# Graph attention on one core: a padded K/V table, and three transfers issued after the table's stores

## The reference

```python
q, k, v = x @ Wq + bq, x @ Wk + bk, x @ Wv + bv          # each as (6250, 8, 16)
scores = sum(q[dst] * k[src], -1) * 16 ** -0.5 + (edge_attr @ We + be)
e = exp(scores - segment_max(scores, dst)[dst])
probs = e / (segment_sum(e, dst) + 1e-10)[dst]
agg = segment_sum(probs[:, :, None] * v[src], dst)
out = layernorm(x + agg @ Wo + bo)
```

## Time and profile before

| what | value |
|---|---|
| time, median of 3 runs | 2090.21 us (2089.79 to 2093.34) |
| time of the profiled execution | 2089.85 us |
| its span | 2088.0 us |
| granted TensorE clock over the span | 0.597 |
| busy: PE, DVE, ACT, POOL | 1462.7, 1441.3, 869.7, 1532.9 us |
| gathers (L481) | 1564, mean 968 ns busy |

### The profile page before, as it was taken

How to read it: one execution, slowest core, us unless ns; L and a number is a source line. 1 busy time by engine, 2 the same in 40 slices (tenths; PEclk the granted TensorE clock), 3 DMA queues, 4 the chain that set the end, 5 groups by cost and what they waited for, 6 DMA issues and landing times.

```text
span 2088.0 us, 31893 instructions
## 1 busy us (share of the span) xinstructions
PE 1462.7 (70%) x8917; PEld 921.8 (44%) x8917; DVE 1441.3 (69%) x3420; ACT 869.7 (42%) x3368; POOL 1532.9 (73%) x1578
## 2 busy tenths in 40 slices
PE   5567767667676777767667787776667776768766
PEld 4344544444443544444435454444444443545443
DVE  5466777766766676767667676766676776767766
ACT  0143435444443444344434444443444343434444
POOL 4777777777777777777777777777777777777770
PEclk8555556665656565566555555656565566655555
DMA  7544444444444444444444444444444444444430
GB/s 292 194 126 127 128 152 126 150 127 147 131 133 142 130 150 127 151 129 151 128 150 129 149 128 148 131 132 143 129 151 128 151 127 151 127 152 126 138 116 9
DMA packets 115285, 290.07 MB, mean 139 GB/s; under 512 B 45719, under 2 KB 53644, under 8 KB 108068
## 3 DMA queue, kind: packets, MB, share of 16 engines
q0 software_dynamic: 75072, 205.10, 32.9%
q1 hardware_dynamic: 37324, 76.25, 10.6%
q10 hardware_dynamic: 2712, 6.67, 0.9%
HBM read 276.38 MB, written 11.51 MB: 138 GB/s over the span
## 4 chain that ended last, share of the span: by engine, by line
POOL 71%; issue 23%; PE 2%; DVE 2%; DMA 1%; ACT 0%; ACTq 0%; POOLq 0%; DVEq 0%
POOL kv_buf L481 71%; PE q_banks L1079 1%; DMA kv_table<-kv_buf 1%; DMA kv_buf<-kv_table,src_i 0%; PE ps_t L1079 0%; PE ps_w L1079 0%; DVE wv L779 0%; PE ps_a L1152 0%; DMA bias_row<-in_L_gnn_bv 0%; ACT distance L546 0%; DVE prod L758 0%; DVE seq_f L854 0%; DVE seq_b L859 0%; PE ps_a L1204 0%; PE ps_a L1205 0%
## 5 line engine op out<-in xcount | busy, mean ns | idle before, releaser
L481 POOL DMA_INDIRECT kv_buf<-kv_table,src_i x1564 | 1514.0, 968 | 495.8 <-issue 473.7
L1116 PE MATMUL q_banks<-q_blk,onehot_t 64*128 64x128 f32 x3128 | 433.3, 418 | 525.6 <-DVE prod L758 520.9
L758 DVE TENSOR_TENSOR prod<-q_banks,kv_buf 128x512 f32<-128x512 f32 (+1 forms) x392 | 269.3, 687 | 564.7 <-issue 467.2
L1116 PEld LDWEIGHTS q_banks<-q_blk,onehot_t 64*128 64x128 f32 x3128 | 335.3, 288 | 639.4 <-issue 636.1
L537 ACT ACTIVATE onehot_t<-ps_t 128x256 f32<-128x256 f32 (+1 forms) x392 | 149.2, 380 | 990.4 <-PE ps_t L1102 978.9
L1152 PE MATMUL ps_a<-wv,onehot 128*64 128x136 f32 x3128 | 418.2, 414 | 60.6 <-ACT onehot L552 58.1
L546 ACT ACTIVATE distance<-iota_n,neg_rel 128x64 f32<-128x64 f32 x1564 | 416.2, 341 | 0.0
L1152 PEld LDWEIGHTS ps_a<-wv,onehot 128*64 128x64 f32 x3128 | 267.3, 202 | 154.1 <-ACT onehot L552 87.6
L779 DVE TENSOR_TENSOR wv<-kv_buf,ps_w 128x512 f32<-128x512 f32 (+1 forms) x392 | 264.4, 675 | 6.0 <-PE ps_a L1152 3.8
L769 DVE TENSOR_REDUCE score<-prod 128x32 f32<-128x512 f32 (+1 forms) x392 | 264.9, 676 | 4.0
L552 ACT ACTIVATE onehot<-distance 128x256 f32<-128x256 f32 (+1 forms) x392 | 163.0, 416 | 12.4
(11 more groups left out here) (144 smaller groups left out, 1417.6 us busy)
## 6 DMA issues: line engine op xcount, KB each, us to landing
edge_f<-in_edge_blk SPq DMA_DIRECT2D x55, 1024.0 KB, 6.2
kv_buf<-kv_table,src_i POOLq DMA_INDIRECT x1564, 3.7
kv_table<-kv_buf ACTq DMA_DIRECT2D x12, 512.0 KB, 5.0
xt_blk<-in_x_t SPq DMA_DIRECT2D x114, 32.0 KB, 4.3
out<-y_out SPq DMA_DIRECT2D x114, 32.0 KB
kv_buf<-in_x_perm SPq DMA_DIRECT2D x5, 512.0 KB, 8.8
codes<-code_table SPq DMA_DIRECT2D x108, 10.5 KB
code_table<-kv_buf SPq DMA_DIRECT2D x1, 1344.0 KB, 6.0
```

Of the source, the lines that this page charges most:

```text
L481: pool.indirect_dma_start(kv_buf[:, b % NBUF, t, :], None, kv_table, bass.IndirectOffsetOnAxis(ap=src_i[:, column:column + 1], axis=0)).th ...
L758: dve.tensor_tensor(prod[:, q % 2, 0:n * D].rearrange("p (k j d) -> p j k d", j=2, d=D), q_banks[:, :, 0:n // 2 * D].rearrange("p j (k d) ...
L1116: one = pe.matmul(ps_q[j][:, k * D:(k + 1) * D], onehot_t[own, q % 2, k * P:(k + 1) * P], q_blk[own, b % QBUF, :], start=True, stop=True)
```

## The change

The last group gets 128 nodes in place of 106, so the table has `NR` = 6272 rows; the 22 extra rows hold what zero features give and no edge points at them. The last chunk of x is loaded 640 columns wide in place of 618. On SP the loads and the store behind `src` now wait for all table stores, and stand in another order: order check, code table, distances. POOL no longer waits for the code table before its first gather, but for the codes to be computed; the wait for the code table's store now stands before those steps of block 0 whose tiles lie in the codes' place.

```diff
-    GROUPS += [(n, 1, min(P, N - n), False) for n in range(N // (QUAD * P) * QUAD * P, N, P)]
+    GROUPS += [(n, 1, P, False) for n in range(N // (QUAD * P) * QUAD * P, N, P)]
+    NR = GROUPS[-1][0] + GROUPS[-1][1] * P
...
-    XCHUNKS = [(0, min(N, QUAD * P))] + [(lo, min(N, lo + XCHUNK)) for lo in range(QUAD * P, N, XCHUNK)]
+    XCHUNKS = [(0, min(NR, QUAD * P))] + [(lo, min(NR, lo + XCHUNK)) for lo in range(QUAD * P, NR, XCHUNK)]
...
-        kv_table = nc.dram_tensor("kv_table", [N, KV], F32).ap()
+        kv_table = nc.dram_tensor("kv_table", [NR, KV], F32).ap()
...
-        xt = in_kv(P, 1, 0, N)
+        xt = in_kv(P, 1, 0, NR)
...
-        row_code = kv_buf[0:ROWS, 0, 16:28, :].rearrange(...)
+        CODE_HOME = (16, 28)
+        row_code = kv_buf[0:ROWS, 0, CODE_HOME[0]:CODE_HOME[1], :].rearrange(...)
...
             sync.dma_start(src_i[:, :], src_blk).then_inc(s_src, 16)
+
+            for i in range(STAGES):
+                sync.wait_ge(s_table[i], TABLE_DONE[i])
+            sync.dma_start(chk_i, dst_chk).then_inc(s_chk, 16)
             sync.wait_ge(s_rowcode, ROWCODE["rest"])
             sync.dma_start(code_table.rearrange("k (r e) -> r k e", e=ROW), row_code).then_inc(s_codetable, 16)
-            sync.wait_ge(s_staged, len(HALVES))
-            sync.dma_start(chk_i, dst_chk).then_inc(s_chk, 16)
             sync.dma_start(dst_i[:, :], dst_blk).then_inc(s_dst, 16)
             sync.wait_ge(s_setup, SETUP["codes"])
             sync.wait_ge(s_codetable, 16)
...
             def gather(b):
                 for g, (t0, t1) in enumerate(STEP[b]):
+                    if b == 0 and t0 < CODE_HOME[1] and t1 > CODE_HOME[0]:
+                        pool.wait_ge(s_codetable, 16)
...
             for i in range(STAGES):
                 pool.wait_ge(s_table[i], TABLE_DONE[i])
-            pool.wait_ge(s_codetable, 16)
+            pool.wait_ge(s_rowcode, ROWCODE["rest"])
             gather(0)
...
-         x_t[:, quads:N]], axis=1)
+         x_t[:, quads:N + -N % P]], axis=1)
```

More of the change, by code:

```diff
@@ L165, in graph_attention @@
         found = sb("found", [1, 4])
-        assert T * KV >= N and T >= max(STAGES * QUAD, 16) and 2 * (NT + 1) <= 2 * EPAIRS * P
+        assert T * KV >= NR and T >= max(STAGES * QUAD, 16) and 2 * (NT + 1) <= 2 * EPAIRS * P
         assert ROW + 1 <= 8 * KV and KNOWN * ROW <= 12 * 2 * KV
@@ L173, in in_kv @@
             return kv_buf[0:parts, half, slot:slot + -(-(n + at) // KV), :].rearrange("p a b -> p (a b)")[:, at:at + n]
-        xt = in_kv(P, 1, 0, N)
+        xt = in_kv(P, 1, 0, NR)
         row_i = in_kv(ROWS, 0, 0, ROW + 1).bitcast(I32)
         row_sq = in_kv(ROWS, 0, 8, ROW)
-        row_code = kv_buf[0:ROWS, 0, 16:28, :].rearrange("p a b -> p (a b)").bitcast(BF16)[:, 0:KNOWN * ROW].rearrange(
+        CODE_HOME = (16, 28)
+        row_code = kv_buf[0:ROWS, 0, CODE_HOME[0]:CODE_HOME[1], :].rearrange("p a b -> p (a b)").bitcast(BF16)[:, 0:KNOWN * ROW].rearrange(
             "p (k e) -> p k e", k=KNOWN)
```

## The result

| | before | after |
|---|---|---|
| time, median of 20 runs each | 2090.31 us (2087.79 to 2094.34) | 2082.78 us (2080.29 to 2090.67) |
| ratio | | 0.9966, 95% interval 0.9959 to 0.9973 |
| profiled execution, its span | 2089.85, 2088.0 us | 2082.24, 2080.4 us |
| mean of a gather | 968 ns | 968 ns |
| granted TensorE clock | 0.597 | 0.603 |

A forecast was written before the change was run, and what follows sets the result against it. POOL issuing 1564 gathers in a row was taken as the bound, so the first gather's start counts. Terms -8.2 (start), -0.8 (first gather) and +1.5 (stretch) sum to -7.5 us on 2089.85: 2082.4 us, range 2079.5 to 2088.5.

The forecast's parts named there:

- What bounds the kernel: POOL issuing 1564 gathers one behind another, 1987.7 of 2088.0 us; the change touches the first gather's start.
- Last store and what stands in front: Padded store with transfers behind it lands in 3.3 us, not 11.49; gathers start at 36.5, not 44.66: -8.2 us.
- at worst as the twelfth now: Bound on the last table store: it takes 6.9 us and lands at 38.9, so gathers start only 4.9 us earlier.
- First gather, -0.8: POOL's first gather takes 0.95 us in place of 1.72, as VectorE is then idle and not in L733.
- What runs beside gathers, +1.5: VectorE's L727, L733 and L740, 4.6 us in all, now fall among gathers and stretch them; bounds 0 and 4.6.
- Waits moved on POOL: Code table lands at 43.5 us, gather 17 needs it at 56: 13 us of cover, so no cost.
- Moved on SP: Later check, code table and distances put the flag at 48.4 to 50.6 us, first multiply about 62; no cost.
- The room of 30 us: Slack before POOL waits for a used slot: 40.8 us now, 30 left with earlier gathers and later consumers.
- Late landing: Rival: backlog isn't the code table's alone, table done at 38.9 us; -4.2 us, 2085.7 us; chance 0.12.
- no effect: Rival: the gain at the start is lost before the end, for instance by POOL stalling; 2089 us; chance 0.08.
- full blocking at 4.6 us: Rival: POOL is held for all of L727, L733 and L740; -4.4 us, 2085.4 us; chance 0.12.
- The slower case: Rival: gathers meet VectorE's SBUF instructions in another phase, stretch grows by half, 14 us; 2096.4 us; chance 0.06.

The follow-up runs named there:

- e3: The changed kernel with the code table's store back at its old place at 25 us, check and distances still behind the table; ratio 0.9980 to the kernel before.
- e2: The kernel before with only the transfers moved behind the table stores, the last store keeping its 106 partitions; ratio 0.9966 to the kernel before.
- e9: The changed kernel itself, unedited, run on a chip where the kernel before takes 2644.3 us; ratio 1.0013 to the kernel before.

## Why the prediction was right, point by point

- **What bounds the kernel.** Right: the start of the first gather moved 7.63 us and the span 7.6. The chain is POOL 72% and issue 23%.
- **The sum.** Forecast -7.5, profiled -7.6 us, and that it is so close is luck. The terms were -8.2 (measured -7.63), -0.8 (-0.56) and +1.5 (+1.4), which makes -6.8. The rest came from elsewhere: 0.9 us less stretch in the later gathers, against 0.1 us more tail; neither stood in the sum.
- **Last store and what stands in front.** Right in size: landed 3.40 us after issue, 3.3 forecast. That the store was issued at 32.77 and not 32.32 is scatter of the stage (31.2 to 32.8 in the other profiles). The bound "at worst as the twelfth now" wasn't needed. That the backlog was the code table's above all was wrong: the loads behind it cost the last store more (3.96 against 2.71 us).
- **First gather, -0.8.** Off by 0.2: 1.16 us, not 0.95. All profiles of the changed order have 1.16 or 1.17, so 0.21 us belong to the first gather itself, and only 0.56 of its old 0.77 to L733 (which ended at 45.34: 45.34 + 0.82 + 0.21 = 46.37, measured 46.38).
- **What runs beside gathers, +1.5.** The size was nearly right, 0.98 + 0.40 = 1.4 us, and the way to it wrong. I took a rate from the steady state, 28 us where it is 34.4, and put it on L842 and its neighbours. No gather started well inside L842 itself; the conversion L840 before it makes 7.4 us, the scan L854 21.5. And I used the row at 139.87 against the port rule. With the 0.82 us it fits to the hundredth: 139.81 + 0.39 + 0.82 = 141.02, and 139.87 + 1.16 = 141.03. The Trainium skill, page "SBUF — State Buffer", section "SBUF: two separate sides", says that the port is held for the whole VectorE instruction and GpSimd fully blocked. The runs agree for a gather that starts second: it ends 0.82 us after L733 has ended, here (44.17 us) and in e3 (44.54 us). My rival priced that rule at the sum of the instructions, 4.6 us; but POOL pays only for what is left of an instruction when a gather starts, here 1.4 us of 3.5. A gather that had started first paid nothing.
- **Waits moved on POOL.** Right: the code table landed at 36.56 + 9.1 = 45.7 us, forecast 43.5 (no row stood behind its 1.5 us of latency), and gather 17 starts 1.25 us behind gather 16.
- **Moved on SP.** Forecast flag 48.4 to 50.6, measured 51.2; first multiply 63.94, just over my 61 to 63. The distances took 11.2 us to land, as SP's queue moved 0.25 MB/us at first, where I had 0.36. It cost nothing: the multiplies caught up with the gathers by 85.3 us, and POOL waited 0.9 us for VectorE in the whole run. The room of 30 us was read from the trace and not shown by an experiment.
- **Rivals.** Late landing and no effect are excluded by the chain, full blocking at 4.6 us by the two gathers. The slower case, stretch in another phase, didn't come; but its size is real: e2's stretch is some 7 us more than the changed kernel's.

## What to carry to other kernels

When one engine's row of equal instructions is the whole span, the prize is its first start: look which transfers stand in the DMA engines in front of the one it waits for, and put behind it all that nobody needs yet, by weight. A store whose packets run on only two DMA engines, as this one of 106 partitions, cost 1.05 us by itself and 2.75 us among others. Before counting on such a gain, make sure that the engine is the limit on each chip that will run it: in e9, where it waits for the others anyway, starting earlier showed no gain.

## What the runs showed of the hardware that I had not expected

- A gather issued by GpSimd takes 0.95 us. Where it starts while one of certain VectorE instructions is at work, it ends 0.75 to 0.83 us after that instruction (139 gathers in the kernel before). These are the ones with two SBUF operands, scans among them, and also the conversion L840 and the product L797 with one. VectorE isn't held up in turn: the scan L854 took 1.22 us (median) both in the 27 cases where a gather had started up to 0.6 us before it and in the 13 where none was at work. The gather beside L739 in e3:

```profile
45.45 1.72 DVE L739 TENSOR_TENSOR neg_rel<-base_bc,neg_rel 128x1512 f32<-128x1512 f32 x1
...
46.09 1.90 POOL L487 DMA_INDIRECT kv_buf<-kv_table,src_i  x1 [0.30 <-issue]
```

- The order check's load moved 0.50 MB in 2 us with nothing else in the engines, which were 99.3% busy; between 42 and 44 us, with SP's and POOL's queues at work together, it was 0.84 MB. Why the first is slow is open.
- The same kernel takes 2090, 2644 or 2715 us, by the chip; each chip was used in one stretch of time, so chip and time aren't told apart. In e9's profile POOL's gathers run at their pace while the other engines stand for up to 47 us. The cause is open.
